# Attention stage of a graph network: a one-hot of four visits by one operation on two repeated tensors, or by four operations with one number for each partition

## The reference, cut to what matters

```python
feat = jnp.concatenate([x[src], edge_weights, x[dst]], axis=1)
h = jax.nn.relu(feat @ W_att1.T + b_att1)
scores = (h @ W_att2.T + b_att2)[:, 0]
m = jax.ops.segment_max(scores, src, num_segments=num_nodes)
e = jnp.exp(scores - m[src])
denom = jax.ops.segment_sum(e, src, num_segments=num_nodes)
alpha = e / denom[src]
msg = jax.ops.segment_sum(alpha[:, None] * lin_x[dst], src, num_segments=num_nodes)
```

## Time and profile before

| what | value |
|---|---|
| median of three runs | 8225.21 us (8221.96 to 8228.91) |
| profiled execution, its own time | 8237.49 us |
| its span | 8235.7 us |
| PE busy | 5000.4 us, 61% |
| DVE busy | 4679.1 us, 57% |
| POOL busy | 5010.1 us, 61% |
| ACT busy | 1976.8 us, 24% |
| attention stage | 6030.7 to 8068.0 us |
| L1937 in the stage | 444 times, 306.6 us, mean 690 ns |
| L1922 | 1776 times, 496.7 us, mean 280 ns |

### The profile page before, as it was taken

The page is one execution under the profiler, slowest core; times in us unless marked ns, Lnnn a source line. Parts: engine busy times, 40 slices in busy tenths (PEclk is TensorE's granted clock), DMA queues, the critical chain, the costliest instruction groups (busy, mean ns, idle before and its releaser), DMA issues.

```text
span 8235.7 us, 174817 instructions
## 1 busy us (share of the span) xinstructions
PE 5000.4 (61%) x30075; PEld 3745.0 (45%) x30076; DVE 4679.1 (57%) x20491; ACT 1976.8 (24%) x5537; POOL 5010.1 (61%) x10349
## 2 busy tenths in 40 slices
PE   5433455555533376555555555555568888888885
PEld 2233333333333354444444444444456667677773
DVE  3566677677733374222222222222279999999997
ACT  3000000000000033222222222222235555555553
POOL 0466666666666626666666666666657777777772
PEclk9655555555555577666667676677679999988889
DMA  7222222222222223222222222222233333333332
GB/s 219 49 47 49 46 45 46 44 45 46 45 50 49 49 54 121 89 88 88 87 84 86 84 84 85 85 84 85 84 117 95 95 94 94 94 94 95 95 94 70
DMA packets 1140621, 649.01 MB, mean 79 GB/s; under 512 B 794817, under 2 KB 1044467, under 8 KB 1139700
## 3 DMA queue, kind: packets, MB, share of 16 engines
q1 hardware_dynamic: 1002212, 412.36, 20.6%
q0 software_dynamic: 137728, 233.30, 9.9%
q10 hardware_dynamic: 608, 2.55, 0.1%
HBM read 360.62 MB, written 311.42 MB: 82 GB/s over the span
## 4 chain that ended last, share of the span: by engine, by line
another core or an unknown queue 19%; issue 15%; DVE 7%; POOL 7%; PE 6%; ACT 5%; DVEq 1%; POOLq 1%; ACTq 0%; DMA 0%
PE banks L1299 2%; ACT ring L998 2%; ACT ring L1005 2%; DVE wide L1926 2%; PE banks L1345 2%; DVE wide L1931 1%; DVE ring L1937 1%; POOL ring L867 1%; POOL ring L851 1%; POOL ring L848 1%; DVE acc L1922 1%; POOL ring L846 1%; POOL ring L859 1%; POOL ring L840 1%
## 5 line engine op out<-in xcount | busy, mean ns | idle before, releaser
L806 POOL DMA_INDIRECT rows_by_src<-ring x1760 | 1772.0, 1007 | 1045.3 <-ACT ring L1005 546.0
L778 POOL DMA_INDIRECT wide<-msg_table,ring x1664 | 1647.1, 990 | 1200.4 <-issue 559.9
L1299 PE MATMUL banks<-wide,ring 128*128 x3520 | 1356.7, 515 | 889.7 <-ACT ring L998 639.2
L1299 PEld LDWEIGHTS banks<-wide,ring 128*128 128x128 f32 x3520 | 795.5, 279 | 1149.1 <-issue 1109.3
L1213 PE MATMUL banks<-wide,ring 128*128 x3520 | 860.6, 426 | 567.6 <-DVE acc L1666 192.0
L1213 PEld LDWEIGHTS banks<-wide,ring 128*128 128x128 f32 x3520 | 783.9, 328 | 653.1 <-issue 652.2
L1894 DVE COPY ring<-ring 128x4 f32<-128x4 f32 x440 | 79.5, 181 | 1572.9 <-DMA rows_by_src<-ring 1457.2
L1005 ACT COPY ring<-banks 128x416 f32<-128x416 f32 x880 | 406.7, 520 | 2070.8 <-remote 1607.5
L1666 DVE TENSOR_TENSOR acc<-acc,banks 128x64 f32 x1760 | 389.4, 221 | 835.6 <-issue 331.3
L1345 PE MATMUL banks<-wide,ring 128*128 x5328 | 718.9, 254 | 0.0
L944 ACT COPY ring<-wide 128x4 int32 (+1 forms) x416 | 80.1, 193 | 2558.1 <-DMA wide<-msg_table,ring 2283.0
(11 more groups left out here) (320 smaller groups left out, 9691.5 us busy)
## 6 DMA issues: line engine op xcount, KB each, us to landing
wide<-rows_by_src SPq DMA_DIRECT2D x1776, 105.0 KB, 2.0
ring<-attr_turned SPq DMA_DIRECT2D x440, 128.0 KB
attr_turned<-ring SPq DMA_DIRECT2D x416, 96.0 KB
rows_by_src<-ring POOLq DMA_INDIRECT x1760
wide<-msg_table,ring POOLq DMA_INDIRECT x1664
msg_table<-ring SPq DMA_DIRECT2D x100, 256.0 KB, 2.0
ring<-attr_by_dst SPq DMA_DIRECT2D x208, 64.0 KB
attr_turned<-ring SPq DMA_DIRECT2D x208, 64.0 KB
```

The costliest lines, as they stand in the source:

```text
L778: g.indirect_dma_start(out=A_g[:, b * GV + u, :], out_offset=None, in_=table[:, :], in_offset=bass.IndirectOffsetOnAxis(ap=A_idx[:, s, u:u ...
L806: g.indirect_dma_start(out=rows_d[:, :], out_offset=bass.IndirectOffsetOnAxis(ap=B_pos[:, s, u:u + 1], axis=0), in_=B_row[:, s, u, :], in_ ...
L1299: mm(b, B_DT[:, t, u, :], qh[:, w, :].rearrange("p a k -> p (a k)"), start=True, stop=False)
```

## The change

L1937 compares `iota_b`, repeated for four visits, with the keys, each repeated 128 times: one tensor operation of 512 columns. After the change four operations of 128 columns compare `iota_b` with one number for each partition, column u of the keys. For that the keys are kept in 4 bytes each, and `C_kl` takes 24 columns of the ring in place of 12. The semaphore is raised by the last of the four; the waits in front stay where they are.

```diff
-        C_kl = part(ring, CS * GV // 2, RING).bitcast(bf16).rearrange("p (s u) -> p s u", s=CS)
+        C_kl = part(ring, CS * GV, RING).rearrange("p (s u) -> p s u", s=CS)
@@
-                    v.tensor_tensor(C_N[:, s, :, :], iota_b[:, :].unsqueeze(1).to_broadcast([P, GV, P]),
-                                    per_group(C_kl[:, s, :], P), ALU.not_equal).then_inc(c_N, 1)
+                    for u in range(GV):
+                        m = v.tensor_scalar(C_N[:, s, u, :], iota_b[:, :], C_kl[:, s, u:u + 1], None, ALU.not_equal)
+                    m.then_inc(c_N, 1)
```

## The result

The changed kernel takes 8284.25 us (median of 4 runs, 8276.24 to 8293.37), the kernel before 8227.06 us (4 runs, 8221.96 to 8233.03). The ratio is 1.0070, with a 95% interval of 1.0055 to 1.0086: the change costs 57 us. The forecast was 8281 us, slower.

What follows compares the result with a forecast made beforehand. It took the vector engine's in-order chain as the bound, the register read behind L1937 setting L1922's start in most ticks. Delay 24 plus collisions 32 made +56 us on the 8225 us median: 8281 us, range 8216 to 8345 (0.81).

Steps and rivals of the forecast that it cites:

- Engine time of the four: Vector engine, one-hot: four operations make 0.67 us start to start against 0.60 for one; bounds 0.39 and 1.01 us.
- The queue: Vector engine's queue: three more instructions before the register read, 0.02 us each, move L1922 from 0.74 to 0.80 to 0.81 us.
- Pass-through and collisions: Attention tick: 0.065 us delay in five of six ticks, +24 us; running maximum waits for POOL's L851 in two, +32 us.
- The margin argument: L1967 against POOL's L851: a 0.065 us later start uses up the 0.06 us margin; a colliding tick is 0.22 us longer.
- what a longer first part costs: Tick's chain behind L1922: 0.065 us passes into the tick, except in one of six where the queue runs ahead; +24 us.
- Key and layout: POOL's key in 4 bytes for each value and buffers behind it moved by 48 bytes: costs nothing.
- They don't overlap: Rival, one-hot: the four run without overlap, 1.01 us against 0.74, +120 us, 8345 us; chance 0.10.
- Collisions don't come: Rival, L1967 and L851: the margin moves along, only the delay counts, 8249 us or 8258; chance 0.20.
- Nothing comes through: Rival, vector engine's queue: the hand-overs run under the wait for the key, 8225 us, within 16; chance 0.14.
- Faster: Rival, POOL's L834: four short operations let it in between, up to -19 us, 8206 us; chance 0.12.
- the price of 0.043 us: POOL's L834: most that a tick shortens if it is let in between, from mean 244 ns against median 201.

Runs made afterwards that it cites:

- e4_read_first: The changed kernel with the register read moved in front of the four one-hot operations and their waits: 7257.48 us against 7248.53, ratio 1.0012.
- f1_before_read_first: The kernel before, one one-hot operation, with the register read moved in front of the one-hot's waits: 7250.23 us against 7254.14, ratio 0.9992.
- e2_three_more: The kernel before with three one-column writes that nobody reads between the one-hot and the register read: 7300.08 us against 7248.53, ratio 1.0072.
- e6_sums_later: The changed kernel with the second sum moved behind the long maximum and the last between the two additions: 7278.95 us against 7247.91, ratio 1.0041.
- e3_wide_keys: The kernel before with only the key's buffer widened to 4 bytes for each value, one operation kept: 7249.95 us against 7248.53, ratio 1.0003.
- f3_one_first_and_later: The kernel before, one one-hot operation, with the register read in front and the sums in the later order: 7273.06 us against 7254.14, ratio 1.0028.

## Why the prediction was right, point by point

**The time.** 56 us were forecast, 57 measured. The steps:

*Engine time of the four.* Forecast 0.17 us apart and 0.25 us long, measured 0.163 and 0.248 us; complete after 0.742 us, forecast 0.76. Building the price from a constant, a number and a 16-bit row held. With the read out of the way L1922 stands at 0.66 us, in e4_read_first, against 0.61 in f1_before_read_first.

*The queue.* Forecast 0.02 us for each hand-over and L1922 at 0.80 to 0.81 us; measured 0.823 us in the mean, against 0.754, thus 0.069 us for three, 0.023 each. The mean is right in part by luck, for the terms behind it offset each other. The ticks stand in six fixed places of the loop body, and each place has its own times, nearly the same in each body in the places 1 to 4 of the changed kernel (means of 67 or 68 bodies in us; "to the next" is from the start of the running maximum to the start of the operation behind it):

| tick of the body | L1922 behind the one-hot, before and changed | maximum to the next, before and changed | tick, before and changed |
|---|---|---|---|
| 1 | 0.833, 0.940 | 0.222, 0.221 | 4.580, 4.684 |
| 2 | 0.820, 1.018 | 0.238, 0.577 | 4.639, 4.871 |
| 3 | 0.742, 0.710 | 0.240, 0.238 | 4.443, 4.619 |
| 4 | 0.739, 0.842 | 0.252, 0.506 | 4.481, 4.618 |
| 5 | 0.720, 0.703 | 0.237, 0.237 | 4.352, 4.461 |
| 6 | 0.673, 0.728 | 0.346, 0.261 | 4.856, 4.872 |

In ticks 1, 2 and 4 the read starts behind the wait and 0.10 us later than before, 0.034 us for each of the three hand-overs, where 0.02 was forecast. In ticks 3 and 5, each behind a tick that collides, the queue is ahead and L1922 comes earlier than before, as the prediction said of such a tick. And tick 2 has 0.10 us on top that no term held: the queue's last step before L1922 ends 155 ns ahead of it, against 57 ns in the kernel before. It costs 74 x 0.10 = 7 us if all of it comes through. One such tick of the changed kernel:

```profile
6490.73 0.74 DVE L1938 TENSOR_SCALAR ring<-iota_b,ring 128x128 bf16<-128x128 bf16 x4
...
6491.64 0.19 POOL L840 TENSOR_TENSOR ring<-ring 128x4 bf16<-128x4 f32 x1
6491.75 0.28 DVE L1922 SCALAR_TENSOR_TENSOR acc<-acc,ring,banks 128x65 f32 x1 [0.27 <-issue]
```

L1922 starts 0.11 us behind POOL's L840 here. But that POOL holds it doesn't fit: in e2_three_more the same tick has the same 155 ns on the queue with POOL's operation 0.13 us ahead, and in tick 4 of the changed kernel L1922 starts 0.09 us behind an L840 with the usual 57 ns. What holds it stays open.

*Pass-through and collisions.* Forecast 24 us for the delay and 32 us for collisions, in two of six ticks. Collisions came in 34.5% of the ticks, and the maximum's mean was 359 ns where some 360 were named. They come in ticks 2 and 4 of the body, in every body, and in few others: two of six, as forecast. e6_sums_later, with collisions taken away and a delay kept, is +28 us over its counterpart; by that 57 falls into 28 for the delay (uncertain by some 12) and 29 for collisions (by some 17). That split is an estimate: it was measured in another order of the sums, where the delay was larger. The two kernels' own traces give another one that needs no second order. Of the 0.129 us of the mean tick, 0.069 lie between the one-hot and L1922, 0.085 between the running maximum and the operation behind it, -0.040 in the rest of the chain (behind a collision the rest takes 0.16 to 0.18 us less, why isn't shown), and 0.015 in the idle time in front of the next one-hot. Times 444 that is 31 us for the delay, 20 for collisions with what follows them, and 6 for a key that comes later. Both splits have the delay and the collisions as real terms of like size; the forecast of 24 and 32 has the delay some 7 us too low and the collisions too high by the second split, and the near hit of the sum is in part luck.

What was wrong in this step is how the loss is paid. Collisions do alternate, but the ticks behind them don't fall back to 4.4 us. Tick 3 has no collision and an earlier L1922, and is 0.18 us longer than before, since it waits 0.17 us for POOL's key where it waited 0.01; tick 5 is 0.11 us longer, 0.05 of it idle in front of the next one-hot. A tick that collides is 0.23 or 0.14 us longer itself. So part of the loss is paid in the tick behind a collision, and in tick 3 it is the wait for POOL's key. The margin argument (0.06 us, and three hand-overs use it up) gave the right count, and rightly that a tick without one follows, but not the whole payment.

*The step "what a longer first part costs"* holds one way only. 0.069 us more at the head cost; 0.141 us less gained 4 us or nothing in f1_before_read_first. The text spoke of passing 5/6 of any delay on, and a reader would have expected some 50 us of gain from that edit. The wait for the key took up the gain there (89.8 us against 41.6). That the stage stood at a point where three things end together, the vector engine's chain, the key and L834, is my reading of it; no run moves one of the three alone.

*Key and layout*: nothing, as e3_wide_keys shows.

**The rivals.** "They don't overlap" fell at 0.163 us apart. "Collisions don't come" fell at 34.5%. "Nothing comes through" fell with the interval. "Faster", because L834 is let in between, was the rejected rival, and its first half is real: four operations never hold L834 long. Its mean fell by 12 ns in the changed kernel, since in the kernel before only a quarter of the L834 start early enough in the one-hot to be held, but by 115 to 280 ns in the other four orders, and in two of them the four operations come out faster. That the time follows from L834 is argued and not shown: the five prices don't follow its mean in order, and no run changes L834 alone. Two numbers of this part need a word: L834's mean before is 247 ns, not 244, and its median of 201 ns is the trace's but stands in no row shown; the price of 0.043 us is thereby 0.046.

**The rules.** Neighbouring new operations start 0.163 us apart, with 0.248 us of duration. The section "The DRAIN you can't avoid" of "VectorE: DVE Perf Modes" in the Trainium skill, read alone, would have put them 0.25 us apart (an estimate from their duration); the same page adds that an operation that isn't held by its operands' places starts earlier, which I didn't weigh, and which the trace bears out. For the meetings, the maximum waits for L851 (0.58 us at 7008.61) and L834 for the one operation (6008.29 above). "SBUF — State Buffer", section "Who interferes with whom", of the Trainium skill says that who issues first has the shared ports for its whole instruction, and counts both two inputs in SBUF and the fast form of an operation with one input among those that take them. The trace agrees: beside the four L834 takes up to 291 ns in place of 200, beside the one up to 0.72 us. So four short operations hold POOL for 0.09 us at most, and one long one for up to 0.52 us.

## What to carry to other kernels

Count an operation's neighbours on its own queue: where a register read follows, each instruction in front of it costs the hand-over, 0.03 us here where the queue isn't ahead, for one-column writes as for one-hots, and in a loop of 4.6 us where two engines meet to within 0.1 us that was 57 us of 8227. Don't put such a read in the middle of short operations, since nothing queued behind it starts (+96 us). Where else to put it has to be measured: in front of the wait for the key it took 57 us down to 9 with four operations and gained 4 or nothing with one, and behind work longer than the read (0.34 us) it cost 64 us with one, since other waits came to light. And don't judge a small edit in one order of the loop alone: when two engines meet to within 0.1 us, try the edit together with a shift of what it meets; the version that came out fastest (four operations, read in front, sums later, ratio 0.9986 with an interval of 0.9977 to 0.9995) holds two edits that gain nothing in the kernel before.

## What the runs showed of the hardware

- The vector engine's queue stands still during a register read from its memory: with the read behind the first of four operations the second started 0.05 us behind the end of the read, 0.43 us behind the first in the mean instead of 0.163 us, and the kernel took 96 us more than the one before and 39 us more than the changed one.
- Three more instructions in front of the read, whether one-column writes or one-hots of 128 columns, start it 0.09 to 0.10 us later in the ticks in which the queue isn't ahead.
- Operations with one number for each partition and 16-bit data start 0.163 us apart at 128 columns though each is 0.248 us long; the one operation with two repeated tensors took 693 ns for 512 columns. Four cost 0.05 us more than one until the next operation starts (0.66 against 0.61 us).
- A two-tensor operation of the vector engine and a POOL operation on the same memory exclude each other in both directions: POOL's L834 with its four columns took 492 ns in the mean instead of some 200 in f3_one_first_and_later and ended 0.06 us behind the one-hot, and the running maximum took 0.58 us instead of 0.22 behind L851. Beside the four short operations POOL's L834 was held by 0.09 us at most.
- Two reorderings that cost nothing each cost 19 us together, and in that order the price of the four operations is -28 us instead of +57.
